# Layer 0: half of the query-key products summed on TensorE by accumulating transposes, the maximum taken tile by tile, and the softmax sums put ahead of the first norm's moments

## The reference

```python
qkv = jnp.einsum('bnm,fm->bnf', x, Wqkv).reshape(b, n, 16, -1)   # dh = 8
q, k, v = (qkv[..., :dh], qkv[..., dh:2 * dh], qkv[..., 2 * dh:])
scores = jnp.einsum('bnhd,bngd->bnhg', q, k) / 8.0
attn = jax.nn.softmax(scores, axis=-1)
out = jnp.einsum('bnhg,bngd->bnhd', attn, v).reshape(b, n, -1)
x = _layernorm(x + jnp.einsum('bni,mi->bnm', out, Wproj) + bproj)
...
# layer 0's experts: 8, two of them kept by a top-k of the gate's logits
x = _layernorm(x + experts(x))
# layer 1: causal attention over tokens, then experts over the whole hidden width, each with a norm
```

## Time and profile before

| | us |
| --- | --- |
| median of three runs | 2234.11 (2232.35 to 2235.26) |
| the profiled execution's own time | 2234.54 |
| its span | 2232.8 |
| busy: TensorE | 2053.9 (92%) |
| busy: VectorE | 1781.3 (80%) |
| busy: ScalarE | 1557.9 (70%) |
| busy: GpSimd | 1117.5 (50%) |
| mean granted clock of TensorE | 0.967 |

### The profile page before, as it was taken

How to read it: one execution, slowest core, us unless ns; L and a number is a source line. 1 busy time by engine, 2 the same in 40 slices (tenths; PEclk the granted TensorE clock), 3 DMA queues, 4 the chain that set the end, 5 groups by cost and what they waited for, 6 DMA issues and landing times. The chain is left out here.

```text
span 2232.8 us, 60806 instructions
## 1 busy us (share of the span) xinstructions
PE 2053.9 (92%) x16256; PEld 1529.6 (69%) x16256; DVE 1781.3 (80%) x5918; ACT 1557.9 (70%) x3951; POOL 1117.5 (50%) x2439
## 2 busy tenths in 40 slices
PE   5999999996899999999999999999999993999990
PEld 3666666664677766766776776676777672999990
DVE  6899999993488888888888888888888884777775
ACT  2565656564588777878877887887777872777774
POOL 5777777775123444444344344444434434444444
PEclk7999999999899999999999999999999996999995
DMA  1000000000100000000000000000200001222226
GB/s 35 25 21 28 21 28 21 28 23 21 43 2 2 11 11 4 9 11 9 4 12 11 2 11 11 6 7 11 86 3 12 11 2 37 61 66 65 64 61 226
DMA packets 63638, 62.91 MB, mean 28 GB/s; under 512 B 9834, under 2 KB 58613, under 8 KB 62855
## 3 DMA queue, kind: packets, MB, share of 16 engines
q1 hardware_dynamic: 54906, 42.64, 6.3%
q0 software_dynamic: 8448, 16.93, 2.3%
HBM read 33.17 MB, written 22.69 MB: 25 GB/s over the span
## 5 line engine op out<-in xcount | busy, mean ns | idle before, releaser
L1373 DVE SCALAR_TENSOR_TENSOR restT<-ps_t,leadT 128x512 f16<-128x512 f32 (+1 forms) x768 | 458.7, 597 | 136.0 <-ACT leadT L1300 106.1
L1300 ACT ACTIVATE leadT<-ps_t 128x512 f16<-128x512 f32 (+1 forms) x768 | 402.2, 524 | 138.0 <-PE ps_t L1166 137.0
L1149 PE MATMUL ps_s<-xT_all,qm 128*128 128x512 f32 (+1 forms) x1024 | 489.8, 560 | 0.8 <-ACT qm L1281 0.8
L1166 PEld LDWEIGHTS ps_t<-ident,p 128*128 128x128 f32 x2560 | 316.0, 141 | 233.2 <-issue 169.4
L1166 PE MATMUL ps_t<-ident,p 128*128 128x128 f32 x2560 | 413.4, 276 | 8.0 <-DVE restT L1373 6.3
L1291 ACT ACTIVATE p<-ps_s,neg_max 128x512 f32<-128x512 f32 (+1 forms) x512 | 325.6, 636 | 80.3 <-DVE neg_max L1363 67.4
L1363 DVE CUSTOM_DVE_ANT_0 ps_s<-ps_s,mask 128x512 f32<-128x512 f32 (+1 forms) x512 | 319.9, 625 | 44.4 <-PE ps_s L1149 43.1
L993 POOL CAST v_parts<-v_all 128x36 bf16<-128x36 f32 x256 | 56.9, 222 | 562.8 <-PE ps_o L1180 562.8
L1149 PEld LDWEIGHTS ps_low<-xT_all,qm 128*128 128x128 f32 x1024 | 194.8, 190 | 135.7 <-issue 122.4
L1140 PE MATMUL ps_qm<-xT_all,m_head 128*128 128x512 f32 x512 | 264.2, 598 | 0.3 <-issue 0.3
L262 POOL TENSOR_TENSOR pv_prod<-probs,kv 128x2048 f32<-128x2048 f32 x64 | 259.3, 4072 | 3.8 <-POOL probs L254 2.3
(11 more groups left out here) (222 smaller groups left out, 4198.2 us busy)
## 6 DMA issues: line engine op xcount, KB each, us to landing
row_in<-rows_dram SPq DMA_DIRECT2D x136, 65.0 KB
y<-results SPq DMA_DIRECT2D x16, 512.0 KB, 5.2
xT<-in_xT SPq DMA_DIRECT2D x32, 128.0 KB, 2.1
xres<-in_xT SPq DMA_DIRECT2D x32, 128.0 KB, 2.1
xT_all<-x2T SPq DMA_DIRECT2D x32, 128.0 KB, 2.0
out_x<-x SPq DMA_DIRECT2D x16, 256.0 KB, 3.4
xT_all<-in_wide SPq DMA_DIRECT2D x1, 2760.0 KB
results<-row_out,row_in POOLq DMA_INDIRECT x136
```

Source lines behind the costliest of these rows:

```text
L1149: mm = pe.matmul(ps_s[n], qm[j][:, n * P:(n + 1) * P], xT_all[:, bass.ds(b * S, (n + 1) * P)], start=True, stop=True)
L1166: mm = pe.transpose(ps_t[g][:, at + n * P:at + (n + 1) * P], probs[i][:, n * P:(n + 1) * P], ident[:, :])
L1300: act.activation(leadT[j][g][:, :], ps_t[g][:, 0:width[g]], ACT.Copy, scale=RAISE)\
L1373: dve.scalar_tensor_tensor(out=restT[j][g][:, :], in0=ps_t[g][:, 0:width[g]], scalar=RAISE, in1=leadT[j][g][:, :], op0=ALU.mult, op1=ALU.s ...
```

## The change

- The second tile's query-key products are written in another order: the eight elements of a head apart by 256 elements, so that all 256 scores' first products lie together, then all second ones, and so on. TensorE sums them (`sum_scores`): for each half of 128 scores eight transposes accumulate in PSUM. ScalarE copies the sum, which lies turned, to SBUF (`copy_scoresT`), and TensorE turns it back (`turn_scores`).
- VectorE sums only the first tile's products, now to SBUF. Maximum and shift are done tile by tile, and the first of them waits for the turned scores of the second tile.
- On VectorE `exp_sums` and `exp_recips` are ahead of `moments_1`. On GpSimd `normalise` is ahead of `inverse1`.
- On TensorE `project` is ahead of `turn_gates` and `turn_x2`; the score sums lie between the two qkv matmuls, and `turn_scores` behind the first head sums.
- On ScalarE the copy of turned scores and the second copy of key and value are ahead of the gates; the exponentials are split by tile, the first ahead of `copy_oT`, the second behind it.

```diff
@@ -100,7 +100,7 @@
         kv = [sb(f"kv{j}", [P, 2 * 2 * P]) for j in range(2)]
         qk_prod = sb("qk_prod", [P, 2 * HH * DH])
         pv_prod = sb("pv_prod", [P, 2 * HH * DH])
-        score_max = sb("score_max", [P, 2 * H])
+        scores_0, scoresT, max_1 = sb("scores_0", [P, HH]), sb("scoresT", [P, HH]), sb("max_1", [P, H])
         shifted = sb("shifted", [P, 2 * HH])
         exps = sb("exps", [P, 2 * HH])
         exp_sum, exp_rec = sb("exp_sum", [P, 2 * H]), sb("exp_rec", [P, 2 * H])
@@ -136,6 +136,9 @@
         ps_gden, ps_gw = ps_front[:, 3 * P + 32:3 * P + 34], ps_front[:, 3 * P + 36:3 * P + 40]
         ps_gT = ps_turn[0:E, 2 * P:4 * P]
 
+        ps_scoresT, scores_1 = ps_turn[:, 2 * P:4 * P], ps_scores[:, HH:2 * HH]
+
+        scores, score_max = (scores_0[:, :], scores_1), (ps_scores[:, 0:H], max_1[:, :])
         ps_r2T, ps_v = ps_scores[:, 0:2 * P], ps_turn[:, 0:2 * P]
         ps_x2T, ps_r2 = ps_tail[:, 2 * P:4 * P], ps_tail[:, 0:2 * P]
 
...
@@ -305,10 +309,11 @@
                         .then_inc(xres_biased, 1)
 
                 def step(u, j, part):
+                    if part[2]:
+                        normalise(*before(u, j, 1))
                     if part[3]:
                         inverse1(*before(u, j, 2))
                     if part[2]:
-                        normalise(*before(u, j, 1))
                         pv_products(*before(u, j, 1), 0)
                         pv_products(*before(u, j, 1), 1)
                     if part[4]:
@@ -338,10 +343,34 @@
                         when(pe, oT_sb, s)
                         when(pe, x1T_sb, s)
                         when(pe, v_sb, 2 * (s - 2))
+                        pe.wait_ge(scoresT_sb, min(s + 2, NP) if isinstance(s, int) else s + 2)
                     for g in range(H):
                         mm = pe.matmul(tile(ps_oT, a), tile(pv_prod, a * H + g), ident[:, :],
                                        start=(g == 0), stop=(g == H - 1), is_transpose=True)
                     mm.then_inc(pv_summed, 1)
+
+                def sum_scores(u, j):
+
+                    s = 2 * u + j
+                    pe.wait_ge(qk_multiplied, 2 * (s + 1))
+                    when(pe, x1T_sb, s - 1)
+                    when(pe, gT_sb, s - 2)
+                    when(pe, v_sb, 2 * (s - 3))
+                    products = tile(qk_prod, 1, HH * DH)
+                    for c in range(2):
+                        for d in range(DH):
+                            mm = pe.matmul(tile(ps_scoresT, c), products[:, d * HH + c * P:d * HH + (c + 1) * P],
+                                           ident[:, :], start=(d == 0), stop=(d == DH - 1), is_transpose=True)
+                    mm.then_inc(scoresT_ps, 1)
+
+                def turn_scores(u, j):
+                    s = 2 * u + j
+                    pe.wait_ge(scoresT_sb, s + 1)
+                    when(pe, r2T_sb, s - 2)
+                    when(pe, scores_shifted, 2 * s)
+                    for c in range(2):
+                        mm = pe.transpose(tile(scores_1, c), tile(scoresT, c), ident[:, :])
+                    mm.then_inc(scores_turned, 1)
 
                 def project(u, j):
                     s = 2 * u + j
@@ -440,21 +469,26 @@
                         four_experts(*before(u, j, 2), 0, 1)
                     if part[0]:
                         qkv_products(*before(u, j, -1), 0)
+                    if part[1]:
+                        sum_scores(u, j)
+                    if part[0]:
+                        qkv_products(*before(u, j, -1), 1)
                     if part[2]:
                         sum_heads(*before(u, j, 1), 0)
-                    if part[0]:
-                        qkv_products(*before(u, j, -1), 1)
+                    if part[1]:
+                        turn_scores(u, j)
                     if part[3]:
                         four_experts(*before(u, j, 2), 1, 0)
                     if part[2]:
                         sum_heads(*before(u, j, 1), 1)
                     if part[3]:
                         four_experts(*before(u, j, 2), 1, 1)
+                    if part[2]:
+                        project(*before(u, j, 1))
+                    if part[3]:
                         turn_gates(*before(u, j, 2))
                     if part[4]:
                         turn_x2(*before(u, j, 3))
-                    if part[2]:
-                        project(*before(u, j, 1))
                 qkv_products(0, 0, 0)
                 qkv_products(0, 0, 1)
                 steps(pe, step)
@@ -475,13 +509,18 @@
                     when(act, r1_ps, s)
                     act.copy(attnT[:, :], ps_oT).then_inc(oT_sb, 1)
 
-                def exponentials(u, j):
+                def copy_scoresT(u, j):
+                    s = 2 * u + j
+                    act.wait_ge(scoresT_ps, s + 1)
+                    when(act, scores_turned, s)
+                    act.copy(scoresT[:, :], ps_scoresT).then_inc(scoresT_sb, 1)
+
+                def exponentials(u, j, a):
                     s = 2 * u + j
                     when(act, probs_ready, s)
-                    for a in range(2):
-                        act.wait_ge(scores_shifted, 2 * s + a + 1)
-                        act.activation(tile(exps, a, HH), tile(shifted, a, HH), ACT.Exp, scale=0.125)\
-                           .then_inc(exps_ready, 1)
+                    act.wait_ge(scores_shifted, 2 * s + a + 1)
+                    act.activation(tile(exps, a, HH), tile(shifted, a, HH), ACT.Exp, scale=0.125)\
+                       .then_inc(exps_ready, 1)
 
                 def norm1(u, j):
                     s = 2 * u + j
@@ -562,24 +601,27 @@
                         gate_exp(*before(u, j, 2))
                     if part[0]:
                         copy_kv(*before(u, j, -1), 0)
+                    if part[1]:
+                        copy_scoresT(u, j)
+                    if part[0]:
+                        copy_kv(*before(u, j, -1), 1)
                     if part[3]:
                         apply_gates(*before(u, j, 2), 0, 0)
                         apply_gates(*before(u, j, 2), 0, 1)
-                    if part[0]:
-                        copy_kv(*before(u, j, -1), 1)
-                    if part[3]:
                         apply_gates(*before(u, j, 2), 1, 0)
+                    if part[1]:
+                        exponentials(u, j, 0)
+                    if part[2]:
+                        copy_oT(*before(u, j, 1))
+                    if part[1]:
+                        exponentials(u, j, 1)
                     if part[4]:
                         norm2(*before(u, j, 3))
-                    if part[2]:
-                        copy_oT(*before(u, j, 1))
                     if part[3]:
                         copy_gT(*before(u, j, 2))
                         apply_gates(*before(u, j, 2), 1, 1)
                     if part[4]:
                         copy_x2T(*before(u, j, 3))
-                    if part[1]:
-                        exponentials(u, j)
                 copy_kv(0, 0, 0)
                 copy_kv(0, 0, 1)
                 steps(act, step)
@@ -617,10 +659,12 @@
 
                 def qk_products(u, j, a):
                     s = 2 * u + j
-                    when(dve, scores_summed, s)
+                    when(dve, scoresT_ps if a else scores_summed, s)
+                    dve.sem_inc(passed, 1)
                     dve.wait_ge(kv_sb, 2 * s + a + 1)
                     dve.tensor_tensor(
-                        tile(qk_prod, a, HH * DH).rearrange("p (h g d) -> p h g d", h=H, g=H),
+                        tile(qk_prod, a, HH * DH).rearrange(("p (d h g) -> p h g d" if a else "p (h g d) -> p h g d"),
+                                                            h=H, g=H),
                         ps_qkv[a][:, 0:P].rearrange("p (h d) -> p h d", h=H).unsqueeze(2)
                         .to_broadcast([P, H, H, DH]),
                         kv[j][:, 2 * a * P:(2 * a + 1) * P].rearrange("p (g d) -> p g d", g=H)
@@ -667,26 +711,29 @@
                        .then_inc(gates_ready, 1)
 
                 def qk_sums(u, j):
-                    s = 2 * u + j
-                    dve.wait_ge(qk_multiplied, 2 * (s + 1))
-                    when(dve, scores_shifted, 2 * s)
-                    when(dve, r2T_sb, s - 2)
-                    dve.tensor_reduce(ps_scores[:, :], by_head(qk_prod[:, :], DH), AX_X, ALU.add)\
+
+                    s = 2 * u + j
+                    dve.wait_ge(qk_multiplied, 2 * s + 1)
+                    when(dve, scores_shifted, 2 * s - 1)
+                    dve.tensor_reduce(scores_0[:, :], by_head(tile(qk_prod, 0, HH * DH), DH), AX_X, ALU.add)\
                        .then_inc(scores_summed, 1)
 
-                def find_max(u, j):
-                    s = 2 * u + j
-                    dve.wait_ge(scores_summed, s + 1)
```

(36 more changed lines are left out.)

## The result

The changed kernel takes 2260.97 us (median of four, 2260.86 to 2263.69) against 2233.47 for the kernel before in the same comparison: a ratio of 1.0122, 95% interval 1.0109 to 1.0135, 27.5 us longer. Its profiled execution took 2261.01 with a span of 2259.3, 26.5 more than the span before.

A forecast was written before the change was run, and what follows sets the result against it. TensorE's queue was taken to bound the changed kernel: 15.88 - 1.15 + 2.0 + 0.2 + 0.39 + 0.1 = 17.4 us a step. Over 28 steps that adds 43 to 2234.5, giving 2277 us, range 2248 to 2303.

The forecast's parts named there:

- R1: Rival: waits kept on TensorE (0.39 gates, 0.43 x1T, 0.4 switches) partly filled; 2252 us, range 2241 to 2262; chance 0.12.
- (a): VectorE: halving the sum saves 2.2 us, splitting the maximum adds 0 to 0.1; busy time 14.48 to about 12.4.
- (g): VectorE's strided write of second-tile products: 0 us extra, bounds 0 to 2.2; hidden, products ending 2.5 ahead of score sums.
- (b): TensorE: sixteen score-sum transposes cost 1.79 us and two to turn back 0.22, adding 2.0 per step.
- (c): TensorE: 0.2 us for one more switch from matmuls to transposes, 0.1 for eight new queue waits (bounds 0 to 0.3).
- The second loop: Value products, ScalarE's key-value copy, first gates, experts, head sums: 17.0 us long, independent of how full TensorE is.
- R3: Rival: TensorE's line and the second loop delay each other; step 18.2, 2299 us, range 2292 to 2310; chance 0.15.
- (e): TensorE's projection ahead of the gates' transposes: a new 0.39 us stall before the expert sums, no gain possible.
- (f): Exponentials by tile, sums ahead of moments, normalise ahead of inverse: same GpSimd work, 1.30 us inverse now before value products.
- R4: Rival: VectorE's strided product costs over double, say triple; step 19.4, 2333 us; sign: second products over 4.7; chance 0.04.
- R2: Rival, faster: the old loop over GpSimd, projection and moments was the only limit; 14.5 a step, 2196 us; chance 0.03.
- R5: Rival: more transposes lower TensorE's granted clock; at 0.9, a 17.4 us step becomes 19.3, 2331 us; chance 0.03.

The follow-up runs named there:

- e1: Changed kernel with the second tile's products written contiguously like the first's (wrong scores, same instructions): ratio 1.0111, step 16.74 us.
- e3: Changed kernel with each score-sum term added twice on TensorE, 16 more transposes a step: ratio 1.0381, step 18.48 us.
- e2: Changed kernel with only four of the eight score-sum terms added on TensorE, 8 fewer transposes a step: ratio 1.0087, step 16.63 us.
- e5: Changed kernel with ScalarE's second copy of keys and values put back behind the first tile's gates: ratio 1.0130, step 16.73 us.
- e11: Changed kernel with half the score-sum terms left out and ScalarE's second key-value copy behind the first tile's gates: ratio 0.9995, step 15.86 us.
- e4: Changed kernel with the projection put back behind the transposes of gates and x2: ratio 1.0260, step 17.68 us.
- e9: Kernel before with the projection ahead of the gates and x2 transposes and ScalarE's exponentials ahead of the last gates, no TensorE sums: ratio 0.9927, step 15.40 us.
- e7: Kernel before with exponential sums ahead of moments, normalise ahead of inverse, exponentials ahead of the last gates, no TensorE sums: ratio 1.0231, step 17.95 us.
- e10: The e7 kernel with twelve unread identity transposes on TensorE in front of the x1 transposes: ratio 0.9986, step 15.82 us.
- e6: Changed kernel with moments ahead of exponential sums and inverse ahead of normalise again, TensorE's score sums kept: ratio 1.0276, step 17.83 us.
- e8: Kernel before with only the VectorE and GpSimd reorder, ScalarE's exponentials left last, no TensorE sums: ratio 1.0560, step 20.22 us.
- e12: Kernel before with only the projection moved ahead of the gates and x2 transposes, ScalarE's exponentials left last: ratio 1.0081, step 16.49 us.

## Why the prediction was right, and where its steps missed

The direction, the cause and the range held: slower, since TensorE's need rises above the old step. 27.5 us came, 43 were forecast. The time lies below the forecast's own 2265 to 2291 and at the top of what I gave R1 (2241 to 2262). Of R1's three waits that might be filled, both round trips stayed in full (0.91 for x1T, 0.92 from the gates' transposes to the expert sums), but 0.30 of the 0.4 for switches went, so R1 was right in that part. Some of the nearness is luck: the steps brought 22.1, about half of the forecast, and filling and draining, put at 0, added 4.4.

**(a), (g), VectorE, and (d).** The prediction speaks of four-element sums and four terms; each score has eight, and the prices, read from whole rows, don't depend on it. Half of the sum costs 2.29, as estimated (2.2). The maximum by tile costs 0.42 to 0.43 a half, not 0.35 to 0.40. ScalarE's new copy (d) costs 0.37, as said. VectorE's busy time is 14.05 in a step and not about 12.4, most of the difference being the strided write. (g) was mis-sized: I took 0 between bounds of 0 and 2.2 and it is 1.51 (3.74 less 2.23). GpSimd's rows were the wrong ones to go by: there each read at a step of 64 bytes serves eight products in a row, while here every single write of VectorE jumps. That it would be hidden was right: e1 shows 0.0 a step, though the products end 0.9 ahead of the score sums and not 2.5. The Trainium skill ("SBUF — State Buffer", section "Door 1: The DMA port swizzle") says that each access that crosses to a new line pays; the trace agrees, with 1.51 us more for 2048 elements.

**(b), TensorE's load.** Sixteen transposes: 1.79 forecast, 1.74 measured (404.30 to 406.04), and 1.75 by e3. The two of the turn: 0.22 and 0.21. This is the term that carries the result.

**(c), the sum.** 17.4 forecast, 16.8 in the step shown. By group, what was forecast too high: the two passages from qkv to transposes, priced at 0.89 and 0.85, took 0.65 and 0.79 (0.30 together); the 18 + 32 transposes 0.13; the projection took 0.66 and not 0.76; the x1T round trip 0.91 and not 0.97; the new waits nothing and not 0.1; the expert sums 0.02 less. One was too low: the gates' stall took 0.48 and not 0.39. The largest error is the 0.2 in front of the head sums of the earlier trace rows, which I had read as a price of each turn to transposes. Ahead of the score sums it doesn't appear, and ahead of the head sums 0.1 of it is left, so it is no fixed price.

**The second loop.** I put it 0.4 under TensorE's need, with R3 (15%) for the two delaying each other. It is 0.1 under (e2), and the two don't add up: opening it (e5) leaves 16.73 as it was. e11 shows that it is a limit of its own.

**(e), (f), the moves.** The stall for the gates' copy came, 0.48 for 0.39. "No gain is possible, since the projection is no longer on the loop" is the step that failed: e4 puts its worth at 0.95 a step in the changed kernel. The prediction's own times held the answer. They have the value products behind the moved inverse and the moments ending at 2.75, only 0.25 ahead of the end of normalise (3.0), so a projection left 0.44 or more later would have held up the inverse and the value products. In the changed kernel's trace the two ends are as close (414.13 and 414.38).

**Filling and draining.** Forecast 0 within 3 and 0 within 2; measured +6.8 and -2.4, both outside. In step 0 the first maximum of the changed kernel starts at 23.93, before at 22.33: the products are 1.4 longer by the strided write, and the sixteen transposes take 3.47 there (19.17 to 22.64) instead of 1.74. That is half speed, but the granted clock of 18 to 22 us reads 1.00, so its cause isn't shown. In step 2 VectorE waits 5.21 for the turned scores (58.39). They stand in TensorE's queue behind the first head sums and behind four expert matmuls that take 3.76, at a granted clock of 0.50 from 48 to 52 us. I had priced both at full speed.

**The signs.** Of what I said the profile would show, TensorE's busy time is 16.20 a step and not over 16.5, VectorE's idle time 2.76 (16.81 - 14.05) and not over 3, the one as the step is shorter, the other as the strided write is dearer too; the wait ahead of the expert sums is there, and second products last 3.74, under the 4.7 of R4.

**R2 and R5.** R2's condition, TensorE's need under 15.88, is met by no kernel with all of the sums. But its premise, that the old loop over projection and moments set the step, fits e9, which shortens that loop and gains 15 us. R5 had the sign wrong. The granted clock of the changed kernel's steps is 1.00; it is the kernel with fewer transposes and a longer wait (e7) whose clock falls. The Trainium skill ("TensorE: Matmul & The Clock Gate", "Part 4: PE-mode transpose") says that transposes don't count as busy for the clock as other matmuls do. e10 disagrees for this case: twelve transposes, put into the wait, bring the clock of a step from between 0.82 and 0.90 back to 1.00.

What stays open: why e6 costs 1.10 and not 1.6, how e8's loss divides, what slows the first transposes of step 0, and whether e7's order would gain with a shorter wait on TensorE that leaves the clock alone. None of these was followed further.

## What to carry to other kernels

When work is moved from one nearly full engine to another, add up the receiver's queue from start to start, with its round trips, before anything else: where the receiver had 1.1 us of idle time in a step, 1.95 of new work couldn't pay, whatever the giver saved. An instruction moved out of a loop may come back into it through the next one in its engine's queue; follow what it waits for, and what stands behind it. And a wait on TensorE can cost more than its own length: where one grows, look at the granted clock, and judge a reorder with the clock in view.

## What the runs showed of the hardware

- A VectorE multiply of 128 x 2048 in f32 whose innermost output step is 1 KiB takes 3.74 us instead of 2.23, the same inputs and size.
- A wait of 1.26 us on TensorE in front of the x1 transposes of e7 was followed by a stretch at half of the clock (0.53 in the window of 384 to 388 us, 0.62 in the next; four matmuls of 512 columns in 3.76 us instead of 1.96), and waits of that size lowered the clock in each step. Filled with twelve transposes, it stayed at 1.00.
- More idle time in all, in shorter waits, left the clock alone: in e12 TensorE is idle 1.9 us in a step (busy 85.0 of 96 us), no wait between 100 and 500 us is over 0.92, and the granted clock stays at 1.00. In e7 it is idle 1.6 (busy 15.96 of 17.56).
